# Casting the first eight gate/up weight tiles to bfloat16 in DRAM at the start, and loading them with plain transfers from SyncE's queue

## The chip, the cores and the metric

One Trainium2 chip, all 8 cores, one program on each. Every core takes half of the sequence of one batch element (batch 4, two halves). The metric is the device time of the slowest core in microseconds (us). Engines are called as the profile calls them: PE (TensorE), DVE (VectorE), ACT (ScalarE), POOL (GpSimd, which also issues transfers), SP (SyncE, which only issues transfers).

## The reference, cut to what matters

```
x = L0_attn_x                                   # (4, 2048, 2048) float32
x = x + layernorm(attn(layernorm(x)))           # attn: x_proj = x @ Win.T; delta = softplus(x_proj @ B.T)
                                                # a recurrence over the sequence, y = h.sum @ C.T + D*x_proj
                                                # y @ Wout.T, + its input
x = x + layernorm(ffn(layernorm(x)))

def ffn(x):                                     # int8 weights, float32 scales
    gate = silu((x @ w_gate) * s_gate)          # 2048 -> 8192
    up   = (x @ w_up) * s_up                    # 2048 -> 8192
    return ((gate * up) @ w_down) * s_down      # 8192 -> 2048
```

## The kernel before, in words

Everything is kept transposed: 128 features on the partitions, the sequence along the free dimension, 16 feature tiles (DT = 16). A core has TOUT = 1024 columns of its own and PAD = 64 columns ahead of them for the recurrence. The input x sits in SBUF as XT (128 partitions x 16 x 1088 float32, 8.9 MB over three windows of columns: window 2 has 64 columns, windows 0 and 1 have 512 each).

The program is written out by hand: a Python list for each engine (`plan`), filled in program order by helpers. `P` appends an instruction that raises its engine's counter, `DMA(queue, ...)` appends a transfer to the list of the issuing engine, `W` appends a wait, `mm` appends a matmul (all matmuls have line L228). A queue's transfers are issued in the order in which they stand in its list, and a wait in the list holds all that stands behind it.

Stages, in order:
- Loads (L401 to L421). SP issues 13 small constants, the last of them IDENTF, and then the two large windows of XT (each 4 MB, rows of 2 KB). POOL issues window 2 of XT (512 KB), BWTT, the first two tiles of the input projection (WRIT, cast from float32 to bfloat16 on the way), and then 16 casts from DRAM to DRAM: `wout_bf[t] <- w_out_t[t]`, the output projection from float32 to bfloat16, which nobody needs before L764.
- Packs (L430 to L474): DVE and ACT work out powers of sigmoid(A), once the constants have landed.
- First layer norm (`emit_ln`, L479): windows in the order 2, 0, 1. ACT makes a bfloat16 copy (L494) and a square (L496) of each feature tile as it waits for that window of XT, PE sums them over the partitions, a short chain makes mean and 1/sigma, DVE applies them (L582, L585) into XN1T.
- Input projection (L603 to L630): 16 tiles x 3 windows. Tile t+2 is loaded by POOL (L627) after tile t's last matmul.
- Recurrence (packs and shifts, L633 to L756), then the output projection (L757 to L839) with its weight WROT loaded by SP from `wout_bf` (plain copies, two buffers), and three running sums on PE.
- Second layer norm (`emit_ln_chain`, `ln2_combo`, `outer1_apply`), a long chain on DVE.
- Feed forward, twice (k = 0 and 1, 512 columns each): 64 tiles (IT = 64) of gate and up weights, one transfer of 128 x 4096 int8 for both, cast to bfloat16 on the way into SBUF (WGUA for k = 0, WGUB for k = 1, two buffers each). Tiles 0 and 1 are issued at L843, when the output projection is over; tile i+2 at L1074, when tile i's matmuls are over. Each tile is 32 matmuls. Then the down projection, 16 x 4 quarter tiles (WRDAT, WRDBT, L1124), its squares and sums, and the last layer norm.

What stands at the place of the first gate/up load:

```
    v_wgu = {}
    W("gpsimd", t_pe, t_pe.n)
    for i in range(2):
        v_wgu[i] = DMA("gpsimd", s_wrf[i % 2],
                       lambda e, i=i: e.dma_start(out=WGUPW(0, i % 2),
                                                  in_=d_wgu[i]))
```

Of the kernel before, what the change touches and what calls it, by code (L numbers as in the profile page):

```python
# [8 lines left out]
BF16 = mybir.dt.bfloat16  # L9
# [59 lines left out]
def build_program(taps=()):  # L69
    nc = bass.Bass("TRN2", target_bir_lowering=False)  # L70
# [2 lines left out]
    d_win = nc.dram_tensor("w_in_t", [DT, 128, 2048], F32, kind="ExternalInput").ap()  # L73
    d_wout = nc.dram_tensor("w_out_t", [DT, 128, 2048], F32, kind="ExternalInput").ap()
    d_woutb = nc.dram_tensor("wout_bf", [DT, 128, 2048], BF16, kind="Internal").ap()
    d_bwt = nc.dram_tensor("b_w_t", [128, 256], F32, kind="ExternalInput").ap()
    d_cwt = nc.dram_tensor("c_w_t", [16, 2048], F32, kind="ExternalInput").ap()
    d_a = nc.dram_tensor("a_t", [128, 256], F32, kind="ExternalInput").ap()
# [6 lines left out]
    d_wgu = nc.dram_tensor("wgu_t", [IT, 128, 4096], I8, kind="ExternalInput").ap()  # L85
# [10 lines left out]
    for tname, tshape, tdt in taps:  # L96
        tap_out[tname] = nc.dram_tensor("tap_" + tname, tshape, tdt,
                                        kind="ExternalOutput").ap()
# [63 lines left out]
    def Praw(eng, fn):  # L162
        plan[eng].append(fn)

    t_pe, t_vec, t_scl = Trk("t_pe"), Trk("t_vec"), Trk("t_scl")
# [5 lines left out]
    s_wrf = [Trk(f"s_wrf{i}", 16) for i in range(4)]  # L171
    s_wrd = [Trk(f"s_wrd{i}", 16) for i in range(2)]
    s_out, s_tap = Trk("s_out", 16), Trk("s_tap", 16)
    s_wpc = Trk("s_wpc", 16)
    DMAT = ([s_const] + s_x + [s_bwt, s_cwt] + s_wri + s_wro + s_wrf + s_wrd
            + [s_out, s_tap, s_wpc])
    TRKS = [t_pe, t_vec, t_scl] + DMAT
    ETRK = {"tensor": t_pe, "vector": t_vec, "scalar": t_scl}

    def DMA(queue, trk, build):  # L180
        trk.n += trk.step
        plan[queue].append(lambda e, b=build, t=trk: b(e).then_inc(t.h, t.step))
        return (trk, trk.n)

    def W(eng, trk, val=None):
        if val is None:
            trk, val = trk
        if val and val > 0:
            Praw(eng, lambda e, t=trk, v=val: e.wait_ge(t.h, v))

    def P(eng, fn):
        trk = ETRK[eng]
        trk.n += trk.step
        plan[eng].append(lambda e, b=fn, t=trk: b(e).then_inc(t.h, t.step))
        return trk.n
# [162 lines left out]
    def XPBj(j, c0, c1):  # L358
        return XPBT[:, j * T + c0:j * T + c1]
# [7 lines left out]
    def GH(g, c0, c1):  # L367
        return GHT[:, g * 576 + c0:g * 576 + c1]

    def YPRE(t, l0, l1):  # L370
        return YPRET[t][:, l0:l1]
# [46 lines left out]
    for t in range(DT):  # L418
        v_wpre[t] = DMA("gpsimd", s_wpc,
                        lambda e, t=t: e.dma_start(out=d_woutb[t],  # L420
                                                   in_=d_wout[t]))  # L421

    P("vector", lambda e: e.memset(DLY, 0.0))
    v_dly = M("vector")
# [31 lines left out]
    for o in range(1, NO):  # L456
        P("vector", lambda e, o=o: e.tensor_tensor(
            out=pkf4[:, :, o, :], in0=pkf4[:, :, o - 1, :], in1=siga3,
# [119 lines left out]
    def ln1_apply(wi, c0, c1, v_chain):  # L578
        wl = c1 - c0
        W("vector", t_scl, v_chain)  # L580
        for j in range(DT):
# [15 lines left out]
                                        in_=SRA1[0:1, PAD:PAD + 1024]))  # L597
    P("vector", lambda e: e.tensor_copy(out=XROWB[0:1, 0:1024],
                                        in_=SRB1[0:1, PAD:PAD + 1024]))
# [4 lines left out]
    for t in range(DT):  # L604
# [19 lines left out]
        if t + 2 < DT:  # L624
# [3 lines left out]
                                                          in_=d_win[t + 2]))  # L628
# [6 lines left out]
    for wi, (w0, w1) in enumerate(WIN3):  # L635
# [3 lines left out]
        for j in range(DT):  # L639
# [5 lines left out]
            out=SCR[0:16, 0:wl], in_=pb[b][0:16, 0:wl], func=AF.Exp))  # L645
        CB("scalar")
        P("scalar", lambda e, wl=wl: e.activation(
            out=SCR[0:16, 512:512 + wl], in_=SCR[0:16, 0:wl], func=AF.Ln,
# [3 lines left out]
            out=DB[:, w0:w1], in_=SCR[0:16, 512:512 + wl]))  # L652
# [6 lines left out]
    for wi, (w0, w1) in enumerate(WIN3):  # L659
# [7 lines left out]
            out=DR[:, w0:w1], in_=pb[b][:, 0:wl]))  # L667
# [8 lines left out]
    for k in range(2):  # L676
# [4 lines left out]
        for g in range(NG):  # L681
            for pi, (p0, p1) in enumerate(pieces):
# [3 lines left out]
                for j in range(DT):  # L686
# [6 lines left out]
                      out=GH(g, p0 - gb, p1 - gb), in0=pb[b][:, 0:pl],  # L693
# [4 lines left out]
            if g == 0:  # L698
                P("vector", lambda e: e.tensor_copy(
                    out=ACC1[:, 0:519], in_=GH(0, 57, 576)))  # L700
            else:
                c0 = 57 - 8 * g
                P("vector", lambda e, c0=c0, g=g: e.tensor_add(
                    out=ACC1[:, 0:519], in0=ACC1[:, 0:519],
# [11 lines left out]
        for o in range(NO):  # L716
# [5 lines left out]
            out=SHB[:, 512 * k:512 * (k + 1)], in_=pb[b][0:16, 0:512]))  # L722
# [10 lines left out]
    for t in range(DT):  # L733
        for wi in range(2):
# [8 lines left out]
                out=SCR[:, 0:512], in_=XPBj(t, PAD + l0, PAD + l0 + 512),  # L743
# [5 lines left out]
                out=YPRE(t, l0, l0 + 512), in0=pb[b][:, 0:512],  # L749
# [12 lines left out]
    for t in range(2):  # L762
        v_wout[t] = DMA("sync", s_wro[t % 2],
                        lambda e, t=t: e.dma_start(out=WRO(t % 2),  # L764
                                                   in_=d_woutb[t]))
# [8 lines left out]
    for t in range(DT):  # L774
        W("tensor", v_wout[t])
        for wi in range(2):
# [7 lines left out]
            if pend_sum is not None:  # L784
# [5 lines left out]
                out=SQT(sl)[:, 0:512], in_=pb[b][:, 0:512], func=AF.Identity,  # L790
# [5 lines left out]
                out=YATT(t, l0, l0 + 512), in0=SQT(sl)[:, 0:512],  # L796
# [7 lines left out]
                out=d, in_=Xj(t, PAD + l0, PAD + l0 + 512)))  # L804
# [4 lines left out]
                out=SQT(2 + sl)[:, 0:512], in_=YATT(t, l0, l0 + 512),  # L809
# [6 lines left out]
                out=d, in0=s, in1=YATT(t, l0, l0 + 512)))  # L816
# [14 lines left out]
        if t + 2 < DT:  # L831
# [3 lines left out]
                                                           in_=d_woutb[t + 2]))  # L835
# [1 line left out]
    for b_ in (4, 5, 6, 7):  # L837
        banks[b_].w_pe = t_pe.n
    v_wgu = {}  # L839
    W("gpsimd", t_pe, t_pe.n)  # L840
    for i in range(2):
        v_wgu[i] = DMA("gpsimd", s_wrf[i % 2],
                       lambda e, i=i: e.dma_start(out=WGUPW(0, i % 2),  # L843
                                                  in_=d_wgu[i]))
    W("vector", t_pe, t_pe.n)
    P("vector", lambda e: e.tensor_copy(out=SRA[0:1, 0:512], in_=pb[6][0:1, 0:512]))
    P("vector", lambda e: e.tensor_copy(out=SRB[0:1, 0:512], in_=pb[4][0:1, 0:512]))
# [156 lines left out]
    def WGUPW(w, slot):  # L1004
        t = WGUA if w == 0 else WGUB
        return t[:, slot * 4096:(slot + 1) * 4096]
# [5 lines left out]
    for k in range(2):  # L1012
        l0 = 512 * k
        if k == 1:
            W("vector", t_scl, v_combo[1])
            for j in range(DT):
                P("vector", lambda e, j=j, l0=l0: e.tensor_sub(
                    out=SQT(3)[:, 0:512], in0=Xj(j, PAD + l0, PAD + l0 + 512),
# [3 lines left out]
                    out=X2NW(1, j), in0=SQT(3)[:, 0:512], in1=INVB2[:, 0:512]))  # L1022
                v_x2n[(1, j)] = M("vector")
                CB("vector")
        slg = (lambda i: i % 2) if k == 0 else (lambda i: (i + 1) % 2)
        if k == 0:
            pass
        else:
# [4 lines left out]
                                                 in_=d_wgu[1]))  # L1033
        v_fuse_last = 0
        v_scr_gate = t_scl.n
        for i in range(IT):
            W("tensor", v_wgu[i])
            bg = banks[i % 2]
            bu = banks[2 + i % 2]
            pe_acquire(bg)  # L1040
            pe_acquire(bu)
            for j in range(DT):
                if i == 0:
                    W("tensor", t_vec, v_x2n[(k, j)])
                mm(pb[bg.idx][:, 0:512],
                   WGUPW(k, slg(i))[:, j * 128:(j + 1) * 128],
                   X2NW(k, j), j == 0, j == DT - 1)
            bg.w_pe = t_pe.n
            for j in range(DT):
                mm(pb[bu.idx][:, 0:512],  # L1050
                   WGUPW(k, slg(i))[:, 2048 + j * 128:2048 + (j + 1) * 128],
                   X2NW(k, j), j == 0, j == DT - 1)
            bu.w_pe = t_pe.n
            W("scalar", t_pe, bg.w_pe)
            if i == 0:
                W("scalar", t_scl, v_scr_gate)
            if i >= 1:
                W("scalar", t_vec, v_fuse_last)
            P("scalar", lambda e, i=i, b=bg.idx: e.activation(  # L1059
                out=GS, in_=pb[b][:, 0:512], func=AF.Silu,  # L1060
                scale=SGC[:, i:i + 1]))
            vsc = M("scalar")
            bg.r_trk = (t_scl, vsc)
            W("vector", t_scl, vsc)
            W("vector", t_pe, bu.w_pe)
            P("vector", lambda e, i=i, k=k, b=bu.idx: e.scalar_tensor_tensor(  # L1066
                out=FUSE(k, i), in0=pb[b][:, 0:512], scalar=SUC[:, i:i + 1],
                in1=GS, op0=ALU.mult, op1=ALU.mult))
            v_fuse_last = M("vector")
            bu.r_trk = (t_vec, v_fuse_last)  # L1070
            if i + 2 < IT:
                W("gpsimd", t_pe, t_pe.n)
                v_wgu[i + 2] = DMA("gpsimd", s_wrf[slg(i)],
                                   lambda e, i=i, k=k, s=slg(i): e.dma_start(  # L1074
                                       out=WGUPW(k, s), in_=d_wgu[i + 2]))
            if i == 48 and k == 0:
                W("gpsimd", t_pe, t_pe.n)
                for (tt, qq) in [(0, 0), (0, 1)]:
                    v_wd[(tt, qq)] = DMA(
                        "gpsimd", s_wrd[qq % 2],  # L1080
                        lambda e, t=tt, q=qq, k=k: e.dma_start(
                            out=WRDW(k, q % 2),
                            in_=d_wd[t, q // 2, :, (q % 2) * 2048:
                                     (q % 2 + 1) * 2048]))
        if k == 1:
            W("gpsimd", t_pe, t_pe.n)
            W("gpsimd", t_vec, v_fuse_last)
            for (tt, qq) in [(0, 0), (0, 1)]:
# [3 lines left out]
                        out=WRDW(k, q % 2),  # L1092
                        in_=d_wd[t, q // 2, :, (q % 2) * 2048:
                                 (q % 2 + 1) * 2048]))
# [3 lines left out]
        if k == 0:  # L1098
# [3 lines left out]
                                                 in_=d_wgu[0]))  # L1102
# [6 lines left out]
        for t in range(DT):  # L1109
            bk = banks[4 + t % 2]  # L1110
            pe_acquire(bk)
            for q in range(4):
# [7 lines left out]
                if pre[0] < DT and pre not in v_wd:  # L1120
# [4 lines left out]
                            out=WRDW(k, p[1] % 2),  # L1125
                            in_=d_wd[p[0], p[1] // 2, :, (p[1] % 2) * 2048:
                                     (p[1] % 2 + 1) * 2048]))
            bk.w_pe = t_pe.n
            if pend_sum is not None:
# [5 lines left out]
                out=Y2W(k, t), in_=pb[b][:, 0:512], func=AF.Identity,  # L1135
# [3 lines left out]
                out=SQT(sl)[:, 0:512], in_=Y2W(k, t), func=AF.Square))  # L1139
# [14 lines left out]
            out=SRA[0:1, l0:l0 + 512], in_=pb[6 if k == 0 else 7][0:1, 0:512]))  # L1154
        P("vector", lambda e, k=k, l0=l0: e.tensor_copy(
            out=SRB[0:1, l0:l0 + 512], in_=pb[0 if k == 0 else 1][0:1, 0:512]))
# [133 lines left out]
```

## Time and profile before

| what | us |
|---|---|
| median of the 2 runs shown | 2268.01 |
| the 2 runs | 2184.31 and 2351.7 |
| the profiled execution, its own time | 2182.82 |
| span of its slowest core (core 4) | 2180.8 |
| spans of the 8 cores | 2174.6 to 2180.8 |
| PE busy | 1760.7 |
| DVE busy | 415.2 |
| ACT busy | 335.2 |

The profiled execution stands 2.0 us above its span, and close to the faster of the two runs; the other run and with it the median lie higher. All stages below are read from the profiled execution. Times of the rows count from the start of the span of core 4.

### The profile page before, as it was taken

To read this page: it belongs to the slowest core of one execution; us is meant where nothing else is said; L and a number is where in the kernel's file an instruction comes from. 1 tells how busy PE (TensorE), PEld (TensorE's weight loads), DVE (VectorE), ACT (ScalarE), POOL (GpSimd) and SP (SyncE) were. 2 spreads that over 40 slices of the span, in tenths; PEclk is the share of its full clock that TensorE was granted. 3 is DMA by queue.
4 is the path that set the end of the run, shared out by engine and by line. 5 is a ranking of instruction groups with operands and counts; after the bars stand their busy time and mean duration, and the time that the engine had idled before them with its cause. 6 is when DMAs were issued, how large, how long until landed. Compare 5 with 4: busy or idle time off the path is not lost.

```text
span 2180.8 us, 21058 instructions; the slowest of 8 cores (2174.6 to 2180.8 us)
## 1 busy us (share of the span) xinstructions
PE 1760.7 (81%) x8199; PEld 750.1 (34%) x8199; DVE 415.2 (19%) x705; ACT 335.2 (15%) x563; POOL 153.9 (7%) x295
## 2 busy tenths in 40 slices
PE   0066989399504999999999999799999999799980
PEld 0002444033201444444443333244444444333330
DVE  0353003412486111111100000311111111500005
ACT  0371220444301001111100000011111101100010
POOL 1000000000000000000001111000000000111110
PEclk9977999599756999999999999799999999999995
DMA  9911410011101333344433333144444433543332
GB/s 120 164 60 30 77 30 2 19 51 67 59 0 39 151 149 149 150 154 173 155 135 135 135 135 130 69 151 152 154 154 155 154 149 123 180 140 139 129 106 77
DMA packets 52020, 245.62 MB, mean 113 GB/s; under 512 B 6067, under 2 KB 6452, under 8 KB 35284
## 3 DMA queue, kind: packets, MB, share of 16 engines
q0 software_dynamic: 40000, 218.78, 31.0%
q1 hardware_dynamic: 11924, 25.50, 3.6%
q8 instruction: 68, 1.11, 0.2%
q14 instruction: 28, 0.23, 0.0%
HBM read 152.12 MB, written 16.78 MB: 77 GB/s over the span
## 4 chain that ended last, share of the span: by engine, by line
PE 70%; DVE 11%; DMA 9%; ACT 3%; issue 3%; another core or an unknown queue 3%; DVEq 0%; ACTq 0%; POOLq 0%
PE pb L228 70%; DMA WRDBT<-wd_t 4%; DMA WRDAT<-wd_t 4%; ACT SCRT L742 1%; DVE SCRT L946 1%; DVE XT L949 1%; DVE SQT L582 1%; DVE YPRE L748 1%; DVE SQTT L943 1%; DVE XN1T L585 1%; DVE PKF L470 1%; DMA WGUB<-wgu_t 1%; DVE SQTT L954 1%; DVE SCRT L981 1%
## 5 line engine op out<-in xcount | busy, mean ns | idle before, releaser
L228 PE MATMUL pb<-X2NAT,WGUA 128*128 128x512 bf16 x2048 | 445.7, 381 | 91.1 <-DVE SCRT L910 70.1
L228 PE MATMUL pb<-X2NBT,WGUB 128*128 128x512 bf16 x2048 | 449.9, 382 | 14.6 <-DVE X2NBT L1021 13.8
L228 PEld LDWEIGHTS pb<-X2NAT,WGUA 128*128 128x128 bf16 x2048 | 201.1, 98 | 336.0 <-issue 96.8
L228 PEld LDWEIGHTS pb<-X2NBT,WGUB 128*128 128x128 bf16 x2048 | 200.7, 98 | 263.8 <-issue 25.7
L228 PE MATMUL pb<-FUSETB,WRDBT 128*128 128x512 bf16 x1024 | 232.1, 383 | 26.2 <-DMA WRDBT<-wd_t 25.3
L228 PE MATMUL pb<-FUSETA,WRDAT 128*128 128x512 bf16 x1024 | 227.6, 379 | 16.9 <-DMA WRDAT<-wd_t 15.0
L1059 ACT ACTIVATE SCRT<-pb,SGC 128x512 f32<-128x512 f32 x128 | 88.0, 687 | 831.6 <-PE pb L228 803.3
L228 PE MATMUL pb<-SQTT,ONESB 128*1 128x512 bf16 (+1 forms) x160 | 60.3, 436 | 118.9 <-ACT SQTT L494 100.9
L228 PEld LDWEIGHTS pb<-FUSETB,WRDBT 128*128 128x128 bf16 x1024 | 96.9, 98 | 161.0 <-issue 56.1
L228 PEld LDWEIGHTS pb<-FUSETA,WRDAT 128*128 128x128 bf16 x1024 | 96.5, 97 | 148.1 <-issue 40.2
L228 PE MATMUL pb<-XN1T,WRIT 128*128 128x512 bf16 (+1 forms) x768 | 122.5, 323 | 20.4 <-DVE XN1T L585 20.3
L228 PE MATMUL pb<-YPRE,WROT 128*128 128x512 bf16 x512 | 118.1, 385 | 6.7 <-DVE YPRE L748 6.7
L1066 DVE SCALAR_TENSOR_TENSOR FUSETB<-pb,SUC,SCRT 128x512 bf16<-128x512 f32 x64 | 48.1, 751 | 394.9 <-PE pb L228 394.9
L1066 DVE SCALAR_TENSOR_TENSOR FUSETA<-pb,SUC,SCRT 128x512 bf16<-128x512 f32 x64 | 48.1, 751 | 384.3 <-PE pb L228 383.1
L1153 DVE CAST SRNT<-pb 1x512 bf16<-1x512 f32 x2 | 1.4, 678 | 480.0 <-PE pb L228 480.0
L228 PEld LDWEIGHTS pb<-XN1T,WRIT 128*128 128x128 bf16 x768 | 58.6, 99 | 84.9 <-issue 27.1
L228 PEld LDWEIGHTS pb<-YPRE,WROT 128*128 128x128 bf16 x512 | 48.1, 99 | 75.1 <-issue 23.2
L1074 POOL DMA_DIRECT2D WGUA<-wgu_t x62 | 32.7, 528 | 510.0 <-PE pb L228 510.0
L1074 POOL DMA_DIRECT2D WGUB<-wgu_t x62 | 32.7, 528 | 418.0 <-PE pb L228 418.0
L228 PEld LDWEIGHTS pb<-SQTT,ONESB 128*1 128x1 bf16 x160 | 10.7, 81 | 148.8 <-issue 148.8
L228 PE MATMUL pb<-XPBT,PKT 128*128 128x64 bf16 (+1 forms) x384 | 50.1, 295 | 0.7 <-ACT DRT L666 0.7
L1124 POOL DMA_DIRECT2D WRDBT<-wd_t x62 | 32.7, 528 | 225.4 <-PE pb L228 225.4
(129 smaller groups left out, 758.4 us busy)
## 6 DMA issues: line engine op xcount, KB each, us to landing
WGUA<-wgu_t POOLq DMA_DIRECT2D x64, 1024.0 KB, 4.9
WGUB<-wgu_t POOLq DMA_DIRECT2D x64, 1024.0 KB, 4.9
WRDAT<-wd_t POOLq DMA_DIRECT2D x64, 512.0 KB, 3.4
WRDBT<-wd_t POOLq DMA_DIRECT2D x64, 512.0 KB, 3.4
WRIT<-w_in_t POOLq DMA_DIRECT2D x16, 512.0 KB, 5.9
wout_bf<-w_out_t POOLq DMA_DIRECT2D x16, 512.0 KB, 51.0
XT<-xT SPq DMA_DIRECT2D x2, 4096.0 KB, 106.6
WROT<-wout_bf SPq DMA_DIRECT2D x16, 512.0 KB, 3.2
```

The costliest lines, as they stand in the source:

```text
L228: e.matmul(o, l, r, start=st, stop=sp))
L470: P("vector", lambda e: e.tensor_mul(out=PKF, in0=PKF, in1=S8R))
L582: P("vector", lambda e, j=j, c0=c0, c1=c1, wl=wl: e.tensor_sub(out=SQT4[:, 0:wl], in0=Xj(j, c0, c1), in1=MB1F[:, 0:wl]))
L585: P("vector", lambda e, j=j, c0=c0, c1=c1, wl=wl: e.tensor_mul(out=XN1j(j, c0, c1), in0=SQT4[:, 0:wl], in1=INV1B[:, 0:wl]))
L742: P("scalar", lambda e, t=t, l0=l0: e.activation(out=SCR[:, 0:512], in_=XPBj(t, PAD + l0, PAD + l0 + 512), func=AF.Copy, scale=DCOL[:, t:t ...
L748: P("vector", lambda e, t=t, l0=l0, b=bk.idx: e.tensor_add(out=YPRE(t, l0, l0 + 512), in0=pb[b][:, 0:512], in1=SCR[:, 0:512]))
L943: P("vector", lambda e, j=j, c0=c0, wl=wl, src=src: e.tensor_sub(out=SQT(3)[:, 0:wl], in0=src, in1=MB_B[:, 0:wl]))
L946: P("vector", lambda e, j=j, c0=c0, wl=wl: e.tensor_mul(out=CH2[:, 0:wl], in0=SQT(3)[:, 0:wl], in1=INVB[:, 0:wl]))
L1059: P("scalar", lambda e, i=i, b=bg.idx: e.activation(out=GS, in_=pb[b][:, 0:512], func=AF.Silu, scale=SGC[:, i:i + 1]))
L1066: P("vector", lambda e, i=i, k=k, b=bu.idx: e.scalar_tensor_tensor(out=FUSE(k, i), in0=pb[b][:, 0:512], scalar=SUC[:, i:i + 1], in1=GS, op ...
L1074: lambda e, i=i, k=k, s=slg(i): e.dma_start(out=WGUPW(k, s), in_=d_wgu[i + 2]))
L1124: lambda e, p=pre, k=k: e.dma_start(out=WRDW(k, p[1] % 2), in_=d_wd[p[0], p[1] // 2, :, (p[1] % 2) * 2048: (p[1] % 2 + 1) * 2048]))
```

## The change

Eight more transfers from DRAM to DRAM stand behind the 16 of the output projection on POOL's queue: tiles 0 to 7 of the gate/up weights are cast from int8 to bfloat16 into a new DRAM tensor (`wgu_bf`, 8 x 128 x 4096). The loads of tiles 0 to 7 of the first half (k = 0) are then plain copies of 1 MB from that tensor, issued by SP and not by POOL; tiles 8 to 63, and all of k = 1, stay as they were. The two new semaphores for SP's loads and the one for the casts change nothing else.

```
+    d_wgub = nc.dram_tensor("wgu_bf", [8, 128, 4096], BF16, kind="Internal").ap()
...
+    v_wgpre = None
+    for i in range(8):
+        v_wgpre = DMA("gpsimd", s_wgc,
+                      lambda e, i=i: e.dma_start(out=d_wgub[i],
+                                                 in_=d_wgu[i]))
...
-    W("gpsimd", t_pe, t_pe.n)
+    W("sync", t_pe, t_pe.n)
+    W("sync", v_wgpre)
     for i in range(2):
-        v_wgu[i] = DMA("gpsimd", s_wrf[i % 2],
+        v_wgu[i] = DMA("sync", s_wrfs[i % 2],
                        lambda e, i=i: e.dma_start(out=WGUPW(0, i % 2),
-                                                  in_=d_wgu[i]))
+                                                  in_=d_wgub[i]))
...
             if i + 2 < IT:
-                W("gpsimd", t_pe, t_pe.n)
-                v_wgu[i + 2] = DMA("gpsimd", s_wrf[slg(i)],
-                                   lambda e, i=i, k=k, s=slg(i): e.dma_start(
-                                       out=WGUPW(k, s), in_=d_wgu[i + 2]))
+                if k == 0 and i + 2 < 8:
+                    W("sync", t_pe, t_pe.n)
+                    v_wgu[i + 2] = DMA("sync", s_wrfs[slg(i)],
+                                       lambda e, i=i, s=slg(i): e.dma_start(
+                                           out=WGUPW(0, s),
+                                           in_=d_wgub[i + 2]))
+                else:
+                    W("gpsimd", t_pe, t_pe.n)
+                    v_wgu[i + 2] = DMA("gpsimd", s_wrf[slg(i)],
+                                       lambda e, i=i, k=k, s=slg(i):
+                                       e.dma_start(out=WGUPW(k, s),
+                                                   in_=d_wgu[i + 2]))
```

POOL's queue, from the start of the program to the gate/up loads of the first half, before (`wout_bf` is the output projection's bfloat16 copy in DRAM):

```order
5 L411 DMA XT<-xT 128x16x64
6 L412 DMA BWTT<-b_w_t 128x256
7 L416 DMA WRIT<-w_in_t 128x2048 x2
8 L420 DMA wout_bf<-w_out_t 16x16384 x16
9 L627 DMA WRIT<-w_in_t 128x2048 x14
10 L712 DMA CWTT<-c_w_t 16x2048
11 L843 DMA WGUA<-wgu_t 128x4096 x2
12 L1074 DMA WGUA<-wgu_t 128x4096 x49
```

and the same stretch in the changed kernel (its line numbers are 2 to 16 higher):

```order
5 L413 DMA XT<-xT 128x16x64
6 L414 DMA BWTT<-b_w_t 128x256
7 L418 DMA WRIT<-w_in_t 128x2048 x2
8 L422 DMA wout_bf<-w_out_t 16x16384 x16
9 L427 DMA wgu_bf<-wgu_t 16x32768 x8
10 L634 DMA WRIT<-w_in_t 128x2048 x14
11 L719 DMA CWTT<-c_w_t 16x2048
12 L1090 DMA WGUA<-wgu_t 128x4096 x43
```

The eight casts stand between the 16 older ones and WRIT's third tile, with no wait ahead of them; POOL's two loads at L843 and six of those at L1074 are gone.

SP's queue, from the last constant to the end, before:

```order
13 L401 DMA IDENTF<-ident_f 128x128
14 L411 DMA XT<-xT 128x16x512 x2
15 L764 DMA WROT<-wout_bf 128x2048 x2
16 L834 DMA WROT<-wout_bf 128x2048 x14
17 L993 DMA out_xT<-XT 2048x1x512 x2
```

and in the changed kernel:

```order
13 L403 DMA IDENTF<-ident_f 128x128
14 L413 DMA XT<-xT 128x16x512 x2
15 L771 DMA WROT<-wout_bf 128x2048 x2
16 L841 DMA WROT<-wout_bf 128x2048 x14
17 L851 DMA WGUA<-wgu_bf 128x4096 x2
18 L1083 DMA WGUA<-wgu_bf 128x4096 x6
19 L1001 DMA out_xT<-XT 2048x1x512 x2
```

The eight plain loads stand behind the output projection's weights and ahead of the first store of the output; what stands ahead of them, the two windows of XT among it, is as it was.

## Rows read from the trace of the kernel before

**Rows 1.** The page: tenths busy in 40 slices of 54.5 us, DMA share and GB/s
```profile
PE   0066989399504999999999999799999999799980
...
DMA  9911410011101333344433333144444433543332
GB/s 120 164 60 30 77 30 2 19 51 67 59 0 39 151 149 149 150 154 173 155 135 135 135 135 130 69 151 152 154 154 155 154 149 123 180 140 139 129 106 77
```

**Rows 2.** Waits, all of the span: us in total, times, longest us
```profile
PE pb L228 <- ACT SQTT L494: 100.9, 8, 98.2
...
ACT SCRT L430 <- DMA IDENTF<-ident_f: 56.4, 1, 56.4
```

**Rows 3.** ACT's timeline, 106 to 112 us: start, us, then idle time before
```profile
108.54 0.24 ACT L570 CAST INV1B<-SCRT 128x64 bf16<-128x64 f32 x1
109.96 0.62 ACT L494 CAST SQTT<-XT 128x512 bf16<-128x512 f32 x1 [1.17 <-DMA XT<-xT]
```

**Rows 4.** The chain that ended last, 0 to 210 us and on: start, us
```profile
7.28 56.26 another core or an unknown queue
...
108.78 1.04 another core or an unknown queue
...
110.48 0.63 ACT SQTT L496
...
187.72 34.93 PE pb L228 x224
222.74 80.92 PE pb L228 x517
```

**Rows 5.** DMA queues, 20 to 40 us: packets, MB, share of 16 engines
```profile
q0 software_dynamic: 136, 2.23, 100.2%
q1 hardware_dynamic: 136, 0.02, 1.0%
```

**Rows 6.** DMA queues, 60 to 80 us
```profile
q0 software_dynamic: 127, 2.06, 91.8%
q1 hardware_dynamic: 128, 0.26, 6.7%
```

**Rows 7.** DMA queues, 0 to 91 us
```profile
q0 software_dynamic: 1071, 10.00, 93.3%
q1 hardware_dynamic: 1588, 0.79, 4.9%
```

**Rows 8.** DMA queues, 95 to 110 us
```profile
q1 hardware_dynamic: 2176, 4.42, 95.7%
...
q0 software_dynamic: 1, 0.00, 0.0%
```

**Rows 9.** DMA queues, 700 to 1100 us (gate/up tiles)
```profile
q0 software_dynamic: 8368, 59.90, 39.4%
```

**Rows 10.** The page's DMA issues: KB each, us from issue to landing
```profile
WGUA<-wgu_t POOLq DMA_DIRECT2D x64, 1024.0 KB, 4.9
...
wout_bf<-w_out_t POOLq DMA_DIRECT2D x16, 512.0 KB, 51.0
XT<-xT SPq DMA_DIRECT2D x2, 4096.0 KB, 106.6
WROT<-wout_bf SPq DMA_DIRECT2D x16, 512.0 KB, 3.2
```

**Rows 11.** DMA issues: the stores of the output
```profile
out_xT<-XT SPq DMA_DIRECT2D x2, 4096.0 KB, 16.2
```

**Rows 12.** Busy time of a window, 700 to 1100 us: length, PE busy, PEld, DVE, ACT, POOL
```profile
700.00:1100.00 400.00, 398.11 (x1836) 180.14 (x1837) 45.01 (x60) 39.85 (x58) 31.13 (x59) 0.99 0.40 150
```

**Rows 13.** Waits, 665 to 740 us, of PE
```profile
PE pb L228 <- DVE SCRT L910: 70.1, 1, 70.1
PE pb L228 <- DVE FUSETA L1066: 21.0, 1, 21.0
```

**Rows 14.** POOL's timeline, 570 to 700 us: gate/up tiles 0 to 3 of the first half
```profile
574.45 0.55 POOL L843 DMA_DIRECT2D WGUA<-wgu_t  x1 [195.52 <-PE pb L228]
575.23 0.53 POOL L843 DMA_DIRECT2D WGUA<-wgu_t  x1 [0.22 <-issue]
674.57 0.53 POOL L1074 DMA_DIRECT2D WGUA<-wgu_t  x1 [98.81 <-PE pb L228]
681.47 0.53 POOL L1074 DMA_DIRECT2D WGUA<-wgu_t  x1 [6.38 <-PE pb L228]
```

More of the change, by code:

```diff
@@ L173, in build_program @@
     s_out, s_tap = Trk("s_out", 16), Trk("s_tap", 16)
-    s_wpc = Trk("s_wpc", 16)
+    s_wpc, s_wgc = Trk("s_wpc", 16), Trk("s_wgc", 16)
+    s_wrfs = [Trk(f"s_wrfs{i}", 16) for i in range(2)]
     DMAT = ([s_const] + s_x + [s_bwt, s_cwt] + s_wri + s_wro + s_wrf + s_wrd
-            + [s_out, s_tap, s_wpc])
+            + [s_out, s_tap, s_wpc, s_wgc] + s_wrfs)
     TRKS = [t_pe, t_vec, t_scl] + DMAT
```

## The prediction

> **What bounds the kernel now.** I read the page's 40 slices first. From the fifth slice or so PE is busy nearly throughout, and the holes in its row are known chains; but in the first two slices PE does nothing while the DMA row stands at 9, at only 120 and 164 GB/s [rows 1]. The waits say what PE stands for there: 98.2 us for the first square and copy of XT, and ACT before that 56.4 us for the last constant [rows 2]. So the beginning is bound by transfers, and everything behind it hangs on PE.
>
> Next comes the handover to the first layer norm. ACT ends the chain of the small window at 108.78 us and then idles 1.17 us until window 0 of XT is there, at 109.96 [rows 3]. The chain that ended last runs through that wait (it calls it an unknown queue), then through the layer norm, and from 187.72 us through the input projection's matmuls without a gap [rows 4]. So window 0 is already the last to come, by a little, and a later landing of it goes one for one into the end. Nothing behind has slack to swallow it: the later stages wait for each other, not for a point in time.
>
> Then the queues. In 20 to 40 us POOL's queue (q0, the 16 casts of the output projection) has 136 packets and SP's (q1) 136; in 60 to 80 us 127 and 128 [rows 5, 6]. The 16 DMA engines take one packet from each in turn. But a packet of q0 carries 2.23 MB / 136 = 16.4 KB as written, one of q1 at most 2 KB. So while casts are under way SP's loads trickle: 0.79 MB in 91 us [rows 7]. As soon as the casts are through, q1 moves 4.42 MB in 15 us, 295 GB/s [rows 8]. That is why a window of XT takes 106.6 us to land [rows 10]. Whatever is added to POOL's queue behind those casts holds window 0 back further.
>
> The Trainium skill says the same of the arrangement ("DMA: Bandwidth & Descriptors", Queues, rings and completion order): each engine takes its rows in turn, a whole packet at a time; and further on, that issuing from several engines saves only issue time. By that rule, which speaks against this change, an unneeded early cast is not hidden by having its own queue; the trace agrees (127 to 128).
>
> **What the plain loads can bring: nothing, at most 2 us.** Tiles 0 and 1 are issued at 574.45 and 575.23 us and land 4.9 us later [rows 14, 10], while PE waits 70.1 us for the second layer norm [rows 13]. They have some 85 us to spare. Tiles 2 and 3 are issued at 674.57 and 681.47, and PE then waits 21.0 us for DVE anyway [rows 13, 14]. Tiles 4 to 7 have the period of a tile, 6.9 us (681.47 - 674.57), against 4.9 us to land. In 700 to 1100 us PE is busy 398.11 of 400 us [rows 12]: 2 us is all that any load there could give back. The plain copy of 1 MB: a plain 512 KB lands in 3.2 us [rows 10]; another 512 KB at 295 GB/s adds 1.8, so 5.0 us, still under 6.9. If this cover went, each of the six loads could cost its excess; at twice 5.0 us that would be 6 x 3.1 = 19 us, but nothing else is on the engines then. SP's wait for the casts is over some 400 us before it is reached. Behind it on SP stand only the output's stores, far off. POOL loses eight issues of 0.5 us, which were waiting time anyway. I put all of this at 0.
>
> **What the casts cost.** Eight casts read 0.52 MB and write 1.05 MB each: 4.19 MB read, 8.39 MB written, 12.58 MB through DRAM. The trace has no cast from int8 between two places in DRAM. The nearest rows are the casts from float32 in front of them. In 20 to 40 us they write 2.23 MB, so 111.5 GB/s, and read twice that: 334 GB/s together [rows 5]. I take bytes read plus written as the measure: 12.58 MB / 334 GB/s = 37.6 us.
>
> Why this value: plain reads of DRAM make 295 GB/s [rows 8], so 334 looks like what one core gets of DRAM with all cores busy, in whichever direction. As a cross-check I add the two directions one after the other: reads at 295, writes at 4.19 MB in 16.2 us = 259 GB/s [rows 11]. For the old casts that gives 16.8/0.295 + 8.39/0.259 = 57 + 32 = 89 us where the measured rate gives 25.2 / 0.334 = 75; for the new ones 14 + 32 = 47 us, and scaled by the same 75/89, 39 us.
>
> The Trainium skill ("HBM Reference", Access) gives a core about 358 GB/s when both cores of a pair stream. Here 334 GB/s was measured; by the page's figure the casts would take 35 us, an estimate, and the sum would be 2.5 us smaller.
>
> Both ends for this unknown. Low: in the gate/up stage the same cast, from DRAM to SBUF, writes 59.90 MB at a share of 39.4% of 400 us [rows 9], 59.90 / (0.394 x 400) = 380 GB/s as written; 8.39 / 0.380 = 22.1 us. High: if written bytes (or elements, the same number, 4.19 million in each batch of casts) decide, it is the old rate of 111.5 GB/s: 75.2 us. The old casts, between the same places, are the nearer row; both ends stay for the range.
>
> Now SP's packets in between. From 20-40 to 60-80 us the turn of one engine grows from 20/(136/16) = 2.35 us to 20/(127/16) = 2.52 us [rows 5, 6], as SP's packets grow from constants to rows of XT: 0.17 us for a 2 KB packet. The new casts write 8.39 MB / 16.4 KB = 512 packets, 32 on each engine, so 32 x 0.17 = 5.4 us for SP. They carry 512 x 2 KB = 1.05 MB of XT, which is not to be moved later: 1.05 / 0.295 = 3.6 us off. Net +1.8 us. (Were the packets twice as large, it is half of that.)
>
> Landing of window 0, and with it everything behind: +37.6 + 1.8 = +39.4 us. The rest of the beginning is not touched: the constants (ACT gets the last at 7.28 + 56.26 = 63.5 us [rows 4]) and the small window come while the old casts run, the new ones stand behind these; WRIT's first two tiles stand ahead of all casts; its third is issued only after the first tile's matmuls (behind 187.72 us), when the new casts are over (about 91 + 43 = 134 us). Window 1 stands behind window 0 on the same queue and shifts with it; today ACT reaches it only after window 0, with no wait.
>
> Sum: 2182.8 (the profiled execution's own time) + 39.4 + 0 = 2222 us. The median of the runs shown, 2268, mixes that level with one run at 2351.7; I compare with 2182.8. The change is +1.8%. About 2%, 44 us or a time of 2226.5, is what a measurement of this kernel can tell from no change.
>
> **Rivals.**
> 1. *Written bytes or elements set the pace of a cast in DRAM.* +75.2 + 1.8 = 77 us: 2260, slower by 3.5%. For it: nothing in the trace separates reads from writes in the old casts. Against: stores alone make 259 GB/s [rows 11], more than twice 111.5. It decides once the eight casts take more than 42 us.
> 2. *The casts run at the rate of the loads into SBUF.* +22.1 + 1.8 = 24 us: 2207. For it: the same cast, 8 KB packets, 380 GB/s [rows 9]. Against: those casts touch DRAM only to read, at half of that; here 380 GB/s written would come with 190 read, 570 together against the 334 seen [rows 5]. The same page of the Trainium skill on DMA (Anatomy of one DMA) counts written bytes at 436 GB/s, an estimate of 19 us for these casts by it; rows 5 contradict that for DRAM to DRAM.
> 3. *No cost: window 0 is not held back*, as SP's queue gets its rows through in the turns that shorter cast packets give it more often. Time as before, 2183. For it: turns halve to about 1.3 us, SP's share doubles. Against: at 2 KB a turn 16 engines still move only 25 GB/s, and the work of the casts has to be done by the same engines first; the old casts did just that.
> 4. *The plain loads do help*: POOL's cast loads give back what gaps there are, and the casts cost nothing on some cores. At most -2 us [rows 12], 2181.
>
> **Chances.** The forecast's mechanism with the price by total bytes: 0.72, own range 2213 to 2238; the price's uncertainty (35 to 47 us and more) puts 0.48 of it under 2226.5 and 0.24 over it. Rival 1: 0.12. Rival 2: 0.09. Rival 3: 0.04. Rival 4: 0.03. So faster by over 2%: 0.01; within 2%: 0.48 + 0.09 + 0.04 + 0.02 = 0.63; slower by over 2%: 0.36. The range takes in rival 2 (2207 and a little below) and most of the way to rival 1: 2204 to 2252. Outside stand rivals 3 and 4 and the far end of rival 1, under 2 in 10 together.
>
> **What would show it.** Right: ACT's idle time ahead of the first 128x512 copy of XT (L494; now 1.17 us) grows to some 40 us with XT's transfer named; the input projection's matmuls start near 227 instead of 187.7; q0 is at full share until about 134 us with 512 more packets, and q1 has a packet for each; the gate/up stage has its old length. The first constants still land at 63 us. Wrong: ACT's wait stays near 1 us (rival 3); q0 runs on until 165 us or more (rival 1) or stops by 120 (rival 2); or PE waits for WGUA at tiles 2 to 7.

## The result and the profile after

| what | before | after |
|---|---|---|
| median of the runs, us | 2209.51 (10 runs) | 2234.45 (11 runs) |
| lowest, us | 2181.22 | 2219.37 |
| profiled execution, us | 2182.82 | 2236.38 |
| ratio of the comparison | | 1.0203, 95% interval 1.0163 to 1.0242 |

The change makes the kernel slower by 2%. In some runs one die or both had a lower clock for long stretches, whatever the kernel; the ratio leaves those out.

The page of the changed kernel (40 slices, now of 55.9 us; it answers to [rows 1]):

```profile
PE   0024998759921699999999999789999999889980
...
DMA  9970340001110244443443333324344333353332
GB/s 119 154 212 1 60 74 1 2 29 57 67 38 0 76 156 156 155 155 152 170 151 123 135 138 132 113 101 155 149 155 155 152 151 151 116 186 132 133 113 75
```

PE begins its work later than before (its third slice stands at 2 tenths and not at 6), and the DMA row has a third slice at 7 tenths where it had 1. What stands behind is the old pattern, moved.

The waits in the first 260 us, on core 2, the slowest of this execution (us in total, times, longest):

```profile
ACT SCRT L437 <- DMA IDENTF<-ident_f: 54.4, 1, 54.4
ACT SQTT L501 <- DMA XT<-xT: 39.6, 1, 39.6
```

The constants come as before [rows 2]. The new row is the second: ACT waits 39.6 us for window 0 of XT, where it waited 1.17 us [rows 3]. The rows before are from core 4; on that core the new wait is 37.8 us. Its timeline puts it where the prediction looked for it, at the first 128x512 copy:

```profile
146.40 0.62 ACT L501 CAST SQTT<-XT 128x512 bf16<-128x512 f32 x1 [39.59 <-DMA XT<-xT]
```

The DMA queues while the eight casts run, 95 to 125 us (packets, MB, share of 16 engines):

```profile
q0 software_dynamic: 179, 5.83, 91.8%
q1 hardware_dynamic: 180, 0.37, 8.0%
```

One packet of SP's queue goes for each of POOL's, as in [rows 5, 6]. A packet of the new casts is 5.83 MB / 179 = 32.6 KB as written, twice the old one, and a turn of an engine takes 30 / (179/16) = 2.7 us, hardly more than the old 2.35 to 2.5. So they write 194 GB/s where the old ones wrote 111. A piece with twice the written bytes has half the bytes to read: some 49 KB through DRAM in both.

The chain that ended last, at the input projection (start, us), answers to [rows 4]:

```profile
224.79 50.77 PE pb L230 x320
```

187.72 has become 224.79 on core 2, and 224.61 on core 4: +37 us. Nearly the whole of the loss that the casts make is in it.

The spans of the cores show something else as well:

```profile
core 2: 2234.5 us, clock 0.924
core 3: 2233.5 us, clock 0.924
core 4: 2220.3 us, clock 0.934
core 5: 2219.3 us, clock 0.929
```

Cores 2 and 3 are 14 us longer than the rest. The windows of the output projection show where. Core 2, 480 to 580 us (length, PE busy, PEld, DVE, ACT, POOL, granted clock, DMA share, GB/s):

```profile
480.00:500.00 20.00, 19.34 (x67) 7.07 (x68) 2.55 (x6) 5.81 (x9) 0.00 (x0) 0.72 0.08 27
500.00:520.00 20.00, 20.00 (x78) 7.01 (x77) 3.40 (x8) 7.74 (x12) 0.00 (x0) 0.81 0.15 53
520.00:540.00 20.00, 20.00 (x79) 7.00 (x77) 3.40 (x8) 7.74 (x12) 0.00 (x0) 0.81 0.15 52
540.00:560.00 20.00, 20.00 (x82) 6.89 (x81) 3.40 (x8) 8.07 (x13) 0.00 (x0) 0.84 0.16 53
560.00:580.00 20.00, 20.00 (x95) 7.81 (x95) 4.25 (x10) 9.34 (x15) 0.00 (x0) 1.00 0.24 80
```

and core 4, in two of the same stretches:

```profile
500.00:520.00 20.00, 20.00 (x94) 7.65 (x93) 4.25 (x10) 9.26 (x16) 0.00 (x0) 1.00 0.18 54
520.00:540.00 20.00, 20.00 (x95) 7.66 (x94) 4.26 (x10) 9.46 (x15) 0.00 (x0) 1.00 0.27 78
```

Core 2 does 78 matmuls in a stretch in which core 4 does 94, at a granted clock of 0.81 against 1.00, and its clock is under 1.00 for some 80 us. I call that a dip of the clock on a pair of cores. Three timed runs had a pair of longer cores too (2234.45, 2237.7 and 2240.51 us); five others read 2219.37 to 2222.5. Whether the change causes it was the first question for the experiments.

### The profile page after: what moved, and what is told of

Its sections match the earlier page's. It is cut to its first block, busy times and chain, and to the rows that moved or that the text cites. A ratio compares the mean times of both kernels' runs of the same rounds, so it can differ in the third digit from the quotient of the medians.

```text
span 2234.5 us, 21067 instructions; the slowest of 8 cores (2218.1 to 2234.5 us)
## 1 busy us (share of the span) xinstructions
PE 1780.6 (80%) x8199; PEld 753.7 (34%) x8199; DVE 415.0 (19%) x705; ACT 335.1 (15%) x563; POOL 153.6 (7%) x295
## 4 chain that ended last, share of the span: by engine, by line
PE 70%; DVE 11%; DMA 8%; another core or an unknown queue 4%; ACT 3%; issue 3%; DVEq 0%; ACTq 0%; POOLq 0%
PE pb L230 70%; DMA WRDAT<-wd_t 4%; DMA WRDBT<-wd_t 4%; ACT SCRT L749 1%; DVE SQT L589 1%; DVE XT L957 1%; DVE SCRT L954 1%; DVE YPRE L755 1%; DVE XN1T L592 1%; DVE SQTT L951 1%; DMA WGUB<-wgu_t 1%; DVE PKF L477 1%; DVE SCRT L989 1%; DVE SQTT L962 1%
## 5 line engine op out<-in xcount | busy, mean ns | idle before, releaser
L230 PE MATMUL pb<-YPRE,WROT 128*128 128x512 bf16 x512 | 129.2, 411 | 6.7 <-issue 6.7
L1074 DVE SCALAR_TENSOR_TENSOR FUSETB<-pb,SUC,SCRT 128x512 bf16<-128x512 f32 x64 | 48.0, 750 | 395.0 <-PE pb L230 395.0
L1074 DVE SCALAR_TENSOR_TENSOR FUSETA<-pb,SUC,SCRT 128x512 bf16<-128x512 f32 x64 | 48.0, 750 | 385.7 <-PE pb L230 384.5
```

What stands on the lines that cost most here:

```text
L230: e.matmul(o, l, r, start=st, stop=sp))
```

## The experiments

Two theories stood against each other. Mine: the eight casts cost only by keeping window 0 of XT back, at a price of bytes through DRAM, and the plain loads do nothing. The rivals: part of the loss is the plain loads', the clock's, or contention that comes with the casts wherever they stand; or the price is one of turns and not of bytes.

**The casts alone.** The kernel before, with only this:

```
+    v_wgpre = None
+    for i in range(8):
+        v_wgpre = DMA("gpsimd", s_wgc,
+                      lambda e, i=i: e.dma_start(out=d_wgub[i],
+                                                 in_=d_wgu[i]))
```

> The kernel before plus the eight casts alone; the gate/up loads stay casts on POOL's queue. Theory (the casts hold window 0 of XT back, nothing else matters): ACT's wait for XT at its first 128x512 copy is 37 to 40 us as in the changed kernel, and the time is +38 us over before, ratio 1.017, the same as the whole change. Rival (part of the changed kernel's loss comes from the plain loads or from SP's queue): less than that, near +20 us. It also shows whether the dip of TensorE's clock on one pair of cores in the output projection comes with the casts.

Measured: 2222.59 us median against 2184.03; ratio 1.0178, interval 1.0162 to 1.0195: 39 us. Waits:

```profile
ACT SQTT L500 <- DMA XT<-xT: 40.2, 1, 40.2
```

The casts alone make the whole loss. All spans of the profiled execution lie within 2213.8 to 2221.0 us: no pair of cores dips, though the casts are there. In this comparison none of the runs of before has such a pair of cores either.

**The plain loads alone.** The changed kernel without the casts; SP's loads read a bfloat16 tensor that exists already, and SP's wait for the casts is gone with them (cut to the main lines; tiles 2 to 7 are changed in the same way):

```
-    W("sync", v_wgpre)
...
-                                                  in_=d_wgub[i]))
+                                                  in_=d_woutb8[i]))
```

> The changed kernel without the eight casts; SP loads tiles 0 to 7 of the first half as plain 1 MB copies out of wout_bf, which is bfloat16 already (so the first eight gate/up tiles hold the output projection's weights and that part of the result is another one). Theory: plain loads neither gain nor cost, 0 +- 2 us against before, ratio 0.999 to 1.001, XT's wait 1.2 us. Rival (the plain loads save what the cast loads cost): up to -2 us; rival (they are late): PE waits for WGUA at tiles 2 to 7, up to +19 us.

Measured: ratio 1.0005, interval 0.9995 to 1.0016, so between a gain of 1 us and a loss of 3.5 us. Nothing shows that the loads bring or cost anything, and PE waits for WGUA nowhere. The prediction's 0 stands; there was no gap to fill [rows 12].

**The casts later.** The changed kernel with two waits ahead of the eight casts:

```
+    W("gpsimd", v_xw[0])
+    W("gpsimd", v_xw[1])
     v_wgpre = None
     for i in range(8):
```

> The changed kernel with the eight casts held on POOL until both large windows of XT have landed (about 121 us). Theory (they cost only by standing in XT's way): 0 +- 3 us against before, ratio near 1.000; the casts run from 121 to about 165 us, over before WRIT's third tile is issued at 194. Rival (the casts cost by being there at all, through contention for DRAM or SBUF, or the clock): a good part of the +38 us stays.

Measured: ratio 0.9999, interval 0.9990 to 1.0009. POOL waits for XT, and from 125 to 155 us its queue has the DMA engines to itself:

```profile
POOL wgu_bf L429 <- DMA XT<-xT: 107.7, 1, 107.7
```

```profile
q0 software_dynamic: 198, 6.42, 96.7%
```

The same casts, the same bytes, 214 GB/s written, beside the first layer norm's ACT, DVE and PE, and the time is the same within 2 us. So neither contention with the engines' work nor a clock that comes with the casts takes part: the casts cost by standing in the way of transfers that are waited for.

**Sixteen casts.** As the first run, with `range(16)` and a tensor of 16 tiles:

> The kernel before plus sixteen casts instead of eight (tiles 0 to 15), loads unchanged. Theory (price by bytes through DRAM, one for one into the end): twice the change, +76 us, ratio 1.035, ACT's wait for XT about 76 us; the third WRIT tile is issued some 270 us in, still after the casts. Rival (a fixed part, such as a clock or queue effect, beside a smaller slope): clearly less than twice, +50 to +60 us.

Measured: 2259.87 us, ratio 1.0344, interval 1.0325 to 1.0362: 76 us.

```profile
ACT SQTT L500 <- DMA XT<-xT: 79.8, 1, 79.8
```

Twice the casts, twice the loss (39 and 76), twice the wait (40.2 and 79.8, each on the slowest core of its run). A fixed part that would bring 76 down to 50 or 60 is ruled out; one of a few us isn't, as each ratio is known to some 4 us only.

**The eight casts in small rows.** As the first run, each cast in two halves of the columns. A whole tile lies in DRAM without gaps, so that its rows can be joined (flattened) into long pieces; the rows of half a tile can't. The loop now has 16 steps:

```
-                      lambda e, i=i: e.dma_start(out=d_wgub[i],
-                                                 in_=d_wgu[i]))
+                      lambda e, i=i // 2, c=2048 * (i % 2): e.dma_start(
+                          out=d_wgub[i][:, c:c + 2048],
+                          in_=d_wgu[i][:, c:c + 2048]))
```

> The kernel before plus the same eight casts, each as two transfers of half the columns, so that they are written in rows of 4 KB (128 rows of 2048 elements) and not in flattened pieces of 32.8 KB. Same bytes. Theory A (the price is bytes through DRAM): the casts still take about 42 us plus SP's turns; SP now gets a 2 KB packet for each 4 KB, so most of window 0 is through when the casts end; window 0 lands about 35 to 45 us later than before and the time is +33 to +42 us. Theory B (each turn of POOL's queue costs about the same 2.5 us whatever its size, as the 16 KB and the 33 KB packets both did): 128 packets per engine take over 300 us and the time is +250 us or more.

Measured: ratio 1.0162, interval 1.0118 to 1.0205; ACT waits 38.5 us for XT. Queues, 110 to 130 us:

```profile
q0 software_dynamic: 822, 2.98, 75.9%
q1 hardware_dynamic: 823, 1.68, 37.9%
```

That is 822 packets of 3.6 KB in 20 us, a turn of 20 / (822/16) = 0.39 us, not 2.5: theory B is out. SP again has a packet for each of POOL's, so it now moves 84 GB/s and not 12. The casts write 2.98 MB in 20 us, 149 GB/s where they wrote 194, and window 0 lands as late as with the long pieces, as theory A said.

**The old casts in small rows.** The kernel before, nothing added, its 16 casts each in two halves of 1024 columns:

```
-        v_wpre[t] = DMA("gpsimd", s_wpc,
-                        lambda e, t=t: e.dma_start(out=d_woutb[t],
-                                                   in_=d_wout[t]))
+        for c in (0, 1024):
+            v_wpre[t] = DMA("gpsimd", s_wpc,
+                            lambda e, t=t, c=c: e.dma_start(
+                                out=d_woutb[t][:, c:c + 1024],
+                                in_=d_wout[t][:, c:c + 1024]))
```

> The kernel before with its 16 old casts each as two transfers of half the columns, written in rows of 2 KB instead of pieces of 16.4 KB; nothing added. Theory (turns by packet decide SP's share): a turn is some 0.3 us for the cast's packet and 0.17 us for SP's, so SP moves about 70 GB/s from the start: the constants land by 15 us and not 63, window 0 by about 65 to 75 us and not 110; both queues end near 120 us, so window 1 lands as before or a few us earlier and sets the pace: -10 to -25 us in the time. Rival (SP's share is set by bandwidth or priority and not by packets): constants at 63 us, time unchanged.

Measured: ratio 0.9918, interval 0.9861 to 0.9974. ACT's timeline on core 2, the rows that waited for a transfer:

```profile
22.77 0.42 ACT L432 ACTIVATE SCRT<-SIGA 128x256 f32<-128x256 f32 x1 [15.55 <-DMA IDENTF<-ident_f]
76.14 0.62 ACT L496 CAST SQTT<-XT 128x512 bf16<-128x512 f32 x1 [8.19 <-DMA XT<-xT]
124.18 0.62 ACT L496 CAST SQTT<-XT 128x512 bf16<-128x512 f32 x1 [22.32 <-DMA XT<-xT]
```

and the queues from 20 to 40 us:

```profile
q0 software_dynamic: 821, 1.49, 64.7%
q1 hardware_dynamic: 819, 1.65, 34.7%
```

The constants come at 22.8 us and not at 63.5 (I had said 15), window 0 at 76 and not at 110, and window 1, which nobody waited for before, sets the pace at 124.18. In the kernel before, ACT began it at 137.18 us, so this is 13 us earlier; the ratio says 6 to 30 us. The edit changed the size of POOL's packets (and with it the number of its transfers, 32 for 16), not what SP has to load. One packet for one still goes, and what SP moves in 20 us goes from 0.26 MB, once it loads rows of XT [rows 6], to 1.65 MB. The rival of the expectation, a share set by bandwidth or priority, is out.

**The old casts later.** The kernel before with the two waits of above ahead of its own 16 casts:

> The kernel before with its own 16 casts held on POOL until both large windows of XT have landed; nothing added. Theory (everything in the first 110 us waits for transfers that the casts hold back): the constants land by 15 us, XT by 45 us; the beginning is then bound by the packs and the first layer norm on ACT and DVE, window 0's squares begin near 60 us and not 110, and the time is -45 to -55 us, ratio 0.975 to 0.98. Rival (the start is bound by something else): unchanged. Risk: the casts end near 120 to 125 us, when WRIT's third tile is wanted about 145.

Measured: 2158.0 us median against 2203.09, ratio 0.9803, interval 0.9770 to 0.9836. DMA queue 1 (SP) from 15 to 40 us, and queue 0 (POOL) from 50 to 90 us:

```profile
q1 hardware_dynamic: 4012, 7.76, 96.1%
...
q0 software_dynamic: 270, 4.42, 100.5%
```

XT has landed at 44 us, when POOL's wait for it ends; it came at 310 GB/s, and the casts follow at their old 110 GB/s. The last constant lets ACT go at 18.2 us where it had been 63.6, 45 us earlier, and 45 us is what the time shows. After that the start is bound by ACT and DVE: ACT reaches window 0 at 63.3 us without a wait for XT. Two waits in POOL's list make this version faster than both kernels.

**All 24 casts later.** The changed kernel with the two waits ahead of all its casts:

> The changed kernel with all 24 casts held on POOL until XT has landed. Theory: as the run before it, but the casts go on until some 165 us and WRIT's third tile stands behind them in POOL's queue, so the input projection, which begins near 137 us, waits for it some 10 to 20 us: -30 to -45 us against before. Rival (the eight casts are free once XT is out of their way, even here): the same time as with the 16 late ones.

Measured: ratio 0.9820, interval 0.9769 to 0.9872. One row is new:

```profile
PE pb L230 <- DMA WRIT<-w_in_t: 13.2, 1, 13.2
```

WRIT's third tile stands behind the casts in POOL's queue and PE waits 13.2 us for it, as expected (9.6 to 16.0 us on the eight cores). The ratio alone doesn't tell this run from the one before it: their intervals overlap, and the clock dips blur both. The two traces do. On the six cores that had no dip up to that point in either, the last matmul of the output projection starts 9 to 20 us later here (533.5 to 540.5 us against 520.5 to 524.1). So eight more casts cost as soon as something needed stands behind them.

These four ran on another chip than the first four, and there the dip of the clock was common: six of the seven runs of before read 2201.77 to 2204.79 us, and the seventh 2186.91; in each of the six, one to three pairs of cores are longer than the rest by some 15 to 20 us. In the comparisons on the first chip it came in none, with the casts (2222 and 2260 us) or without them. So the dip doesn't need the change. Whether the change makes it more frequent isn't shown: in the comparison of the whole change it came in 3 of 8 runs of the changed kernel and in none of the 5 of before, and the whole change was not run again after that.

## Which step of the prediction failed, and what held

**The step that failed** is the first term of the sum: 2182.8 us, the time of one execution, was taken as the level of every run, with nothing added for a difference between executions. No reason was given for that nothing. What the runs showed:
- The five compared runs of before do lie there, 2181.22 to 2184.31 us (mean 2183.3).
- The five runs of the changed kernel without a dip lie at 2219.37 to 2222.5 us (mean 2221.5). That is +38.2 us, a ratio of 1.0175, and it is what the forecast of +39.4 us and 1.018 describes.
- The three runs with a dip, 2234.45, 2237.7 and 2240.51 us, are 16 us longer. They lift the mean of all eight to 2227.5 us: +44.2 us, the measured 1.0203. So the missing term is 6 us of the measured 44, and the median of all runs, 2234.45, is itself a run with a dip, 12 us over the forecast.

The forecast put 0.63 on "within 2%" and 0.36 on more. The sum of 39.4 us stood only 4.6 us under that bound of 44, and a term of 6 us decided the side. What sets the dip off stays open.

The choice of the level has a second side. Beside the median of 2268 us that the runs shown had, the number 2222 reads as a gain of 2%, and the kernel became slower by 2%. The prediction says that it compares with 2182.8, and the median of before in the next comparison, 2184.03 us over 19 runs, bears that level out and not 2268. But a reader who takes the number beside the median is sent the wrong way.

That 39.4 us came within 1.2 us of the measured 38.2 is in part luck. The mechanism held at each step, but the price was some 1.6 us too small and SP's term 0.9 us too large, and some 3 us remain that nothing here accounts for.

Step by step:
- *What bounds the start*: right. The constants' wait stayed, ACT's wait for XT grew from 1.17 to 37.8 us on core 4, the core of the rows before, and the eight casts held back behind XT cost nothing.
- *One for one into the end*: right, shown by the wait (40.2, 79.8), the times (+39, +76), and PE's start of the input projection (+37).
- *Plain loads: 0*: right (1.0005). The new loads land in 5.8 us at the median on core 2 (4.8 to 6.0 on the eight cores), 8.7 at worst, where 5.0 was forecast. That is still under the tile's 6.9 us but for single loads, PE waits for none, and the first gate/up stage of core 4 lasts 467 us where it lasted 466.
- *The price, bytes read plus written at 334 GB/s*: right in kind, a little small in size. The term was put at 37.6 us. With SP's 12 GB/s beside them the casts made 5.83 x 1.5 / 30 us = 292 GB/s, and 321 when they ran alone, by which 12.58 MB take 39.2 us. The six mixes of the runs, all traffic of both queues added (reads, writes and SP's loads), come to 335 [rows 5], 331 (old casts late), 304 (the change), 321 (new casts late), 307 (small rows) and 306 GB/s (old casts in small rows), while the written bytes alone go from 75 to 214 GB/s. Rival 1 wanted 111 in all of them, rival 2 wanted 380. One measure that nobody tested is the larger of the two directions instead of their sum: both kinds of cast have 2 bytes one way for 1 the other, so it would have given the same 37.6 us. By it the casts alone come to 214 (new) and 221 GB/s (old), while XT's plain loads, which only read DRAM, make 310; by the sum the three are 321, 331 and 310. That speaks for the sum, but no run was made to decide it.
- *SP's packets between*: wrong in its size. I took 32 turns on each engine; there were 16, since a packet of the new casts is 32.6 KB, the case in the parenthesis of the prediction; so there are 256 more packets and not 512. The net term is then 0.9 us, an estimate, and not 1.8. The casts are over at about 132 us on core 4, where 134 was forecast, and window 0 is there at 146.2 us, 36 us later than before. With 39.2 and 0.9 us the sum would be 40 us, so some 3 us are not accounted for; the handover from one queue to the other is a candidate that I did not resolve.
- *Rival 3* (SP overtakes by its turns): its mechanism is real. With small rows SP gets seven times as much (84 against 12 GB/s). But for the casts that stand behind others its effect on window 0 is nil (ACT waits 38.5 us where it waited 40.2), and only where the first casts in the queue were split did the time fall (window 1 begins 13 us earlier).

The Trainium skill's rule that an engine takes its queues in turn, a packet at a time ("DMA: Bandwidth & Descriptors", Queues, rings and completion order), held in every stretch looked at: 179 to 180, 822 to 823, 821 to 819 packets. In this kernel the packets of the two queues differ up to sixteenfold (32.6 KB against 2 KB), and that explains its slow start.

The Trainium skill's figure of about 358 GB/s for a core while both cores of a pair stream ("HBM Reference", Specifications (TRN2); the prediction names another section) was not reached in any of the six mixes, which came to 304 to 335. In rival 2 the reading of 436 GB/s as a rate of written bytes is mine: the Trainium skill ("DMA: Bandwidth & Descriptors", Anatomy of one DMA) gives it for the bytes of a transfer and names no side.

## What to carry to other kernels

A transfer that nobody needs soon isn't free because it has a queue of its own. Here the engines took turns by packet, and a flattened cast in DRAM had packets of 16 to 33 KB against 2 KB or less of the loads that the start needed. So look at packets and MB of each queue in the first stretch, and hold background transfers until the loads that the start needs have landed. And before a load is made cheaper, look whether anybody waits for it: here PE was busy 398.11 of 400 us, and there was nothing to gain. And before a number is forecast to 1%, look at several executions, core by core: one execution doesn't show how far they differ.

## What the runs showed of the hardware that I had not expected

- A transfer from DRAM to DRAM whose rows are contiguous on both sides goes out in pieces of 16.4 KB (float32 to bfloat16) or 32.6 KB (int8 to bfloat16) as written; cut into column halves, the same bytes go in 1.8 to 3.6 KB per packet. A turn takes from 0.39 to 2.7 us accordingly.
- A pair of cores (0 and 1, 2 and 3, ...) sometimes has a lower granted clock than the others for one stretch, and that costs it 14 to 20 us. In the changed kernel it came right after the recurrence, whose tail runs at a granted clock of 0.50 on all cores: cores 2 and 3 stayed at 0.72 to 0.84 for some 80 us of the output projection, 0.81 in its middle, where the others had 1.00. It isn't bound to that place: in the run with the old casts later, cores 4 and 5 had 0.76 to 0.82 from 1820 to 1980 us, in the last down projection, where core 0 had 0.91 to 1.00. On one chip six of seven runs of the kernel before had pairs of longer cores, on another none of those compared. A comparison at the level of 2% of this kernel is not safe against it. What sets it off stays open.
